# Loading the output projection's inputs during the last attention heads of a perceiver block

## The reference

```python
x = x + xattn(layernorm(x), ctx, ctx, ...)   # 16 heads of 64; out = einsum(attn, Wo) + bo
x = x + attn(layernorm(x), ...)              # 8 heads of 64; 20 rounds of row and column normalisation of the logits
x = x + ffn(layernorm(x), ...)               # 8 experts, top-1 routing with a capacity of 161 rows
```

## Time and profile before

| what | us |
|---|---|
| median of 3 runs | 3321.17 |
| lowest and highest | 3320.79, 3326.48 |
| the profiled execution | 3323.82 |
| its span in the profile | 3322.1 |
| PE busy | 3094.8 (93%) |
| DVE busy | 1755.2 (53%) |
| ACT busy | 1453.4 (44%) |
| POOL busy | 116.5 (4%) |

### The profile page before, as it was taken

The page is one execution under the profiler, slowest core; times in us unless marked ns, Lnnn a source line. Parts: engine busy times, 40 slices in busy tenths (PEclk is TensorE's granted clock), DMA queues, the critical chain, the costliest instruction groups (busy, mean ns, idle before and its releaser), DMA issues. The chain is left out here.

```text
span 3322.1 us, 62803 instructions
## 1 busy us (share of the span) xinstructions
PE 3094.8 (93%) x25686; PEld 2701.5 (81%) x25686; DVE 1755.2 (53%) x3257; ACT 1453.4 (44%) x2994; POOL 116.5 (4%) x87
## 2 busy tenths in 40 slices
PE   6899999999999999999999999999879679869997
PEld 5688888888888888888888888888736579859997
DVE  5355656565565555556555555655523788740001
ACT  3355555555555555555555555555512510011111
POOL 0000000000000000000000000000040320100001
PEclk9899999999999999999999999999989755579998
DMA  7311221121121112112112111211080000217761
GB/s 304 118 40 38 74 63 45 55 76 38 51 74 57 42 57 67 38 51 74 57 44 67 57 51 44 74 43 38 10 192 7 16 33 0 78 50 275 252 238 59
DMA packets 234789, 253.16 MB, mean 76 GB/s; under 512 B 22296, under 2 KB 169912, under 8 KB 234064
## 3 DMA queue, kind: packets, MB, share of 16 engines
q1 hardware_dynamic: 233008, 241.79, 22.8%
q0 software_dynamic: 1280, 4.20, 0.4%
q10 hardware_dynamic: 288, 4.19, 0.3%
HBM read 215.42 MB, written 34.70 MB: 75 GB/s over the span
## 5 line engine op out<-in xcount | busy, mean ns | idle before, releaser
L216 PE MATMUL fills<-wv_group,ctxT_hi 128*128 128x256 f32 x4096 | 799.5, 288 | 1.3 <-DVE ctxT_lo L421 0.6
L224 PE MATMUL fills<-ctxT_hi,wk_pairs 128*128 128x512 f32 x2048 | 704.9, 405 | 0.7 <-DVE keys L436 0.7
L216 PEld LDWEIGHTS fills<-wv_group,ctxT_hi 128*128 128x128 f32 x4096 | 655.3, 191 | 24.2 <-issue 21.0
L436 DVE SCALAR_TENSOR_TENSOR keys<-fills,bk,keys 64x512 fp32r<-64x512 f32 x512 | 383.8, 750 | 412.1 <-ACT keys L353 408.4
L216 PE MATMUL fills<-wv_group,ctxT_lo 128*128 128x256 f32 x2048 | 579.4, 283 | 0.0
L353 ACT ACTIVATE keys<-fills,bk 64x512 fp32r<-64x512 f32 x512 | 350.0, 684 | 408.3 <-PE fills L224 405.0
L224 PEld LDWEIGHTS fills<-ctxT_hi,wk_pairs 128*128 128x128 f32 x2048 | 387.8, 189 | 103.7 <-issue 23.8
L429 DVE TENSOR_TENSOR values<-fills,values 128x512 fp32r<-128x512 f32 x256 | 176.9, 691 | 435.7 <-ACT values L348 435.7
L224 PE MATMUL fills<-ctxT_lo,wk_pairs 128*128 128x512 f32 x1024 | 403.5, 394 | 0.0
L216 PEld LDWEIGHTS fills<-wv_group,ctxT_lo 128*128 128x128 f32 x2048 | 392.7, 192 | 0.0
L473 DVE TENSOR_TENSOR probsT<-probsT_ps,probsT 128x512 fp32r<-128x512 f32 x504 | 348.3, 691 | 66.3 <-ACT probsT L385 57.1
(11 more groups left out here) (211 smaller groups left out, 3105.5 us busy)
## 6 DMA issues: line engine op xcount, KB each, us to landing
e_w<-in_L_ffn_W SPq DMA_DIRECT2D x64, 1024.0 KB, 8.7
ctx_stage<-in_ctx SPq DMA_DIRECT2D x128, 256.0 KB, 2.9
wv_group<-wv_split SPq DMA_DIRECT2D x64, 512.0 KB, 4.6
wk_pairs<-wk_split SPq DMA_DIRECT2D x128, 256.0 KB, 3.2
q<-q_split SPq DMA_DIRECT2D x256, 64.0 KB, 2.7
q_split<-p_qb SPq DMA_DIRECT2D x16, 512.0 KB, 3.5
o_parts<-o_half SPq DMA_DIRECT2D x128, 64.0 KB, 1.5
a_ua<-o_parts SPq DMA_DIRECT2D x32, 256.0 KB, 6.6
```

The lines of the kernel that those rows point to most:

```text
L216: last = nc.tensor.matmul(pJ[:, bank[0], 256 * k:256 * k + 256], c[:, t, s:s + P], wv[:, w, t, :], start=t + n == 0, stop=t == DT - 1 and ...
L224: last = nc.tensor.matmul(pJ[:, bank[0], :], wk[:, p, w, t, :], c[:, t, 512 * j:512 * j + 512], start=t + n == 0, stop=t == DT - 1 and n == 2)
L436: last = nc.vector.scalar_tensor_tensor(out=keys[lo_rows(j), x, 512 * j:512 * j + 512], in0=pJ[DK * a:DK * a + DK, bk_, :], scalar=bk_sb[h ...
```

## The change

The context's place in SBUF becomes a region of its own (`shared`), from which a new class `Early` takes buffers that are used once the last fill has been made: `Wo`, the three raw weights of the self-attention (each in its own buffer now), two buffers of `a_ua` and two of the sums `a_us`. The row scales and `xbv` have places outside of it. SP issues `early_loads` in the last group of heads, and GpSimd adds the first two batches during the heads. In the projection's block the remaining sums are made two batches ahead, and the waits are split accordingly. `q_sb` and `k_sb` move to the next block, since the region is given back only after the projection. Semaphores are cleared, with a barrier, after the logits instead of after the whole self-attention.

```diff
+class Early:
+    def __init__(self, nc, offset, left, sem):
+        at = lambda n, shape, words: nc.alloc_sbuf_tensor_at(n, shape, F32, offset=offset + 4 * words)
+        self.xo = at("a_xo", [P, XH // 2, D], 0)
+        self.w = at("a_w", [P, 3, DT, D], 4096)
+        self.ua = at("a_ua", [P, 2, 2, XH // 2, P], 10240)
+        self.us = at("a_us", [P, 2, XH // 2, P], 14336)
...
+    def add(self, nc, pool, b):
+        pool.wait_ge(self.u_in[b % 2], 64 * (b // 2 + 1))
+        nc.gpsimd.tensor_tensor(self.us[:, b % 2, :, :], self.ua[:, b % 2, 0, :, :], self.ua[:, b % 2, 1, :, :],
+                                ALU.add).then_inc(self.added, 1)
...
                         h = 4 * g + i
+                        if last and g == XG - 1:
+                            early_loads(b, i)
...
+            def early_loads(b, i):
+                if i == 0:
+                    sp.wait_ge(filled, PRO + PER * b + fill_no(16 * XG - 17, True) + 1)
+                    for n in range(2):
+                        sp.wait_ge(o_out[n], 128 * 2 + 16)
+                    for n in range(2):
+                        early.u_load(sp, o_parts, n)
+                    sp.dma_start(early.xo[:, :, :], xo.rearrange("(a u) k d -> (u k) a d", u=2)).then_inc(early.xo_in, 16)
+                    sp.wait_ge(scale_out, 16 * batches)
+                    with nc.allow_non_contiguous_dma(reason="one number per token and head; the bias, once"):
+                        sp.dma_start(early.rs[:, 0:B - 1, :], row_scale[0:B - 1].rearrange("b t h -> t b h")).then_inc(early.rs_in, 16)
+                        sp.dma_start(early.xbv[:, :], x_bv.rearrange("(a u) k -> (u k) a", u=2)).then_inc(early.xo_in, 16)
+                    for n in range(3):
+                        sp.dma_start(early.w[:, n, :, :], aw[n].rearrange("(t p) d -> p t d", p=P)).then_inc(early.w_in, 16)
+                if i >= 2:
+                    sp.wait_ge(early.added, i - 1)
+                    for n in range(2):
+                        sp.wait_ge(o_out[n], 128 * (i + 1) + 16)
+                    early.u_load(sp, o_parts, i)
...
+        @block.gpsimd
+        def _(pool):
+            for b in range(2):
+                early.add(nc, pool, b)
...
                 @block.gpsimd
                 def _(pool):
+                    weights_lo(0)
                     for b in range(B):
-                        pool.wait_ge(u_in[b % 2], 64 * (b // 2 + 1))
-                        if b:
-                            pool.wait_ge(merged, b)
-                        nc.gpsimd.tensor_tensor(us[:, :, :], ua[:, b % 2, 0, :, :], ua[:, b % 2, 1, :, :],
-                                                ALU.add).then_inc(added, 1)
+                        if b + 2 < B:
+                            pool.wait_ge(merged, b + 1)
+                            early.add(nc, pool, b + 2)
...
-                        if b in (3, 5, 7):
+                        if b in (1, 3):
+                            weights_lo((b + 1) // 2)
...
                 @block.scalar
                 def _(act):
-                    act.wait_ge(rs_in, 16)
                     for b in range(B):
+                        act.wait_ge(early.rs_in, 16 if b < B - 1 else 32)
...
+            shared_space.close()
...
+        nc.clear_and_free_semaphores(used)
+        nc.all_engine_barrier()
+        used.clear()
         bo_sb = sb("s_bo", [P, D], F32)
...
-            nc.clear_and_free_semaphores(used)
-            nc.all_engine_barrier()
-            used = []
             weights.make(1)
```

More of the change, by code:

```diff
@@ L23 @@
 EPS = 1e-5
+SBUF_END = 229344
 def new_semaphore(nc, name, used):
@@ L29, in new_semaphore, with u_load, cross_attention @@
     return used[-1]
-def cross_attention(nc, ctx, wk_split, wv_split, q_split, bk, ident, o_parts, row_scale, used, batches=B):
+class Early:
[5 more added lines that the diff above has]
+        self.us = at("a_us", [P, 2, XH // 2, P], 14336)
+        self.rs = left("a_rs", [P, B, XH])
+        self.xbv = left("a_xbv", [P, XH // 2])
+        self.xo_in, self.rs_in, self.w_in, self.added = (sem(n) for n in ("a_xo_in", "a_rs_in", "a_w_in", "a_added"))
+        self.u_in = [sem("a_u_in0"), sem("a_u_in1")]
+    def u_load(self, sp, o_parts, b):
+        for n in range(2):
+            for u in range(2):
+                sp.dma_start(self.ua[DK * u:DK * u + DK, b % 2, n, :, :],
+                             o_parts[b].rearrange("(a u) k t -> u k a t", u=2)[u, DK * n:DK * n + DK, :, :]
+                             ).then_inc(self.u_in[b % 2], 16)
+    def add(self, nc, pool, b):
+        pool.wait_ge(self.u_in[b % 2], 64 * (b // 2 + 1))
+        nc.gpsimd.tensor_tensor(self.us[:, b % 2, :, :], self.ua[:, b % 2, 0, :, :], self.ua[:, b % 2, 1, :, :],
+                                ALU.add).then_inc(self.added, 1)
+def cross_attention(nc, ctx, wk_split, wv_split, q_split, bk, ident, o_parts, row_scale, shared, early, xo, x_bv, aw, used,
+                    batches=B):
     NS = 4
@@ L808, in _ @@
                 def _(sp):
[L809 to L815, removed]
@@ L816, in _, with row @@
-                    u_load(0)
-                    sp.dma_start(xo_sb[:, :, :], xo.rearrange("(a u) k d -> (u k) a d", u=2)).then_inc(xo_in, 16)
+                    def row(out, src, done):
+                        sp.dma_start(out[:, :], src.rearrange("(a d) -> a d", a=1).to_broadcast([P, D])).then_inc(done, 16)
+                    row(xbo, x_bo, xb_in)
+                    for hf in range(2):
+                        sp.dma_start(x1[:, 4 * hf:4 * hf + 4, :], x[4 * hf:4 * hf + 4].rearrange("b p d -> p b d")).then_inc(xs_in, 16)
@@ L824, in _ @@
[L824 to L833, removed]
@@ L834, in _ @@
-                    sp.wait_ge(w_in, 48)
+                    row(bvb, bv, c_in)
+                    for b in range(4, B):
+                        sp.wait_ge(early.added, b - 1)
+                        early.u_load(sp, o_parts, b)
+                    sp.wait_ge(c_in, 48)
                 @block.tensor
@@ L859, in _ @@
                         for a in range(XH // 2):
-                            last = nc.tensor.matmul(pY[:, b % 2, :], oT[:, b % 2, a, :], xo_sb[:, a, :],
+                            last = nc.tensor.matmul(pY[:, b % 2, :], oT[:, b % 2, a, :], early.xo[:, a, :],
                                                     start=a == 0, stop=a == XH // 2 - 1)
@@ L1806, in perceiver @@
         prepare(nc, x, xWq, xbq, xWk, xWv, ident, wk_split, wv_split, q_split, used)
-        cross_attention(nc, ctx_1024, wk_split, wv_split, q_split, xbk, ident, o_parts, row_scale, used)
+        shared_space, small = ExitStack(), ExitStack()
+        shared_space.enter_context(nc.sbuf_tensor("shared", [P, 2 * DT * S], F32, side="right"))
+        shared = SBUF_END - 4 * 2 * DT * S
+        early = Early(nc, shared, lambda n, shape: small.enter_context(nc.sbuf_tensor(n, shape, F32)),
+                      lambda n: new_semaphore(nc, n, used))
+        cross_attention(nc, ctx_1024, wk_split, wv_split, q_split, xbk, ident, o_parts, row_scale, shared, early, xWo, xbv,
+                        (aWq, aWk, aWv), used)
         with ExitStack() as kept:
```

61 lines of the change are left out of this document (27 added, 34 removed).

## The result

The changed kernel takes 3281.13 us (median of 4 runs, 3278.18 to 3285.63), the kernel before 3322.78 on the same chip (4 runs, 3320.79 to 3326.48): a ratio of 0.9875, with a 95% interval of 0.9857 to 0.9892. The profiled execution of the changed kernel took 3278.18 us (span 3276.5, mean clock 0.935; before 3322.1 and 0.930).

A forecast was written before the change was run, and what follows sets the result against it. TensorE was taken to limit the output projection, after three holes left by late transfers. Gains of 12.4 and 5.3 less 4.2 us made 13.5 off 3323.82, 3310.3; set against the median shown, forecast 3308 us, range 3302 to 3316.

The forecast's parts named there:

- the part on the rest: Moved semaphore clearing, ScalarE's weight copies, smaller loads and new buffer places, together taken to cost 0 us.
- The front: Output projection, opening to second spread of scales: loads already there, so 12.4 us gained, bounds 7.1 to 15.1.
- The projections: Eight projections, second spread to last projection's end: no hole left, 67.2 to 61.9 us, gain 5.3 us.
- the row: Output projection's waits: a_oT waited 33.9 us for the sums a_us before; forecast: sums always done before their product.
- The first subtraction ahead of the sum: GpSimd's 4.5 us weight subtraction precedes the third sum, done about 2425; product needs it at 2434, so no loss.
- The stall: Last heads: early loads hold head 11's store, head 13's addition is 5.2 us late, cost 4.2 us, bounds 0 to 8.6.
- the working: Calculation for head 11's store: 7.46 MB at 281 GB/s take 26.6 us, landing at 2402.1; VectorE's slack 1.02 us.
- the rival of no stall: Last heads: loads in by 2397 or passed by the store, all 17.7 us gained, 3303.5 us; chance 0.20.
- The moved barrier: Semaphore clearing moved from self-attention's end to after the first row sums' logarithm: gives and costs 0 to 4.4, taken 0.
- The crawl: Early loads among the heads: short pieces hold the queue at 120 GB/s, 62 us, a loss of 21, 3342 us; chance 0.07.
- The prediction's 281 GB/s: Transfer rate assumed for the 7.46 MB up to head 11's store, from the window at 2468: 26.6 us.

The follow-up runs named there:

- both repairs: Changed kernel with the three raw weights loaded behind batch 2's loads and 192 bytes of padding ahead of probsT: 3270.43 us, ratio 0.9851 to the kernel before.

## Why the prediction was wrong

**The step that failed** is one clause in the part on the rest: "the buffers' new places cost nothing while TensorE is the limit". It took the place of a buffer for something that has no time, and put neither a price nor a bound on it. No rival had it either, so the range was too narrow by the whole effect. It is shown by a pair of runs that change nothing but places: the distance of the change put into before gives 32.5 us, and the old distance put into the change takes the time to 3307.77. That this is 0.2 us from the forecast of 3308 is in part luck: the runs of that kernel spread over 5 us, the kernel before was 2.4 us faster on that chip, and in its trace 4.9 us that nobody forecast (`c_pLT` to the experts, 374.4) stand against 3.2 more up to the last fill (2376.1). The two parts add up: 12.6 + 32.5 = 45.1 us, where the change gained 41.6 and 43.9 in its two comparisons. The clause was also wrong in its reason. TensorE was busy for 1993 of the 2030 us from 250 to 2280, so little stood free to cover a matmul that starts 4 to 7 ns later: 26.1 us of the stretch to the last fill went, where the spacing gives 23 and the clock's falls 4.7.

**The front** was right in kind: 13.7 us gained, 12.4 forecast. ScalarE started 0.03 us after SP's first load (2393.00 against 2392.97) where 0.1 was assumed. From the first spread to the second 9.36 us passed (2394.09 to 2403.45) where 10.6 were forecast, since the low clock cost less: it was there until about 2397, 3 us, and not for 5.4 us of work as before.

**The projections**: 61.2 us without a hole, 61.9 forecast. The sums kept ahead. The waits of the stage show none of `a_oT` for `a_us`, which was the row; GpSimd now waits instead, for VectorE:

```profile
POOL a_us L55 <- DVE a_oT L934: 8.5, 3, 4.2
```

The first subtraction ahead of the sum did no harm, as argued.

**The stall** was the best term: a late addition at head 13, by 5.2 us as forecast and 6.5 as measured, for 4.2 and 4.3 us. A wait longer by 1.3 us at the same cost means that more slack stood behind it than the 1.02 us of the working, so the close agreement is partly luck. The store landed 30.0 us after the last fill's end (2376.8 less 2346.8, by the end of the wait), the working had 29.2 (its 2401.1 lets SP begin 0.1 us after the fill, which it does not say). Part of the mechanism was different: SP came to the store only 20 us after the last fill, since it stood while it issued what is ahead (4.92 us for one load of weights), and the queue then took 9.9 us; the working had put it all on the transfers. The changed kernel without the weights ahead shows no wait at all, so the rival of no stall was a matter of 3 MB.

**The moved barrier** was taken at 0 out of -4.4 to +4.4. At its new place the logarithm of the sums ends at 2569.67 and SP's next load comes at 2571.11:

```profile
2569.41 0.26 ACT L1074 ACTIVATE s_ls<-s_rowsum 128x64 f32<-128x64 f32 x1
2571.11 0.37 SPq L1171 DMA_DIRECT2D s_wo<-in_L_attn_Wo  x1
```

so it costs some 1.4 us there, and the stretch grew by 1.3. At the old place, for the earlier trace rows, 2.9 us now lie between the last scatter's issue and the load, where 4.4 lay:

```profile
2939.75 0.96 POOL L1424 DMA_INDIRECT expert_rows<-g_xn,e_slot  x1 [0.30 <-issue]
...
2943.61 0.34 SPq L1674 DMA_DIRECT2D f_eb<-expert_rows  x1
```

The two about cancel. The 4.9 us of the stretch that holds it are not shown to be the change's: kernels with the old barrier place ranged from 373.7 to 379.3 us there, those with the new one from 374.1 to 377.7. The barrier was not tried by itself, nor were the sums two batches ahead without the early loads.

**The crawl** did not come. The loads ahead of the store, with 7.46 MB, were in after 30.0 us, an average of 249 GB/s. By the transfers' own view, in 40 slices of 1.5 us from 2340, the rate sinks for two slices only, when the row scales in 64-byte pieces and `a_xbv` in 4-byte pieces are under way:

```profile
GB/s 0 0 0 5 0 74 255 201 201 200 208 205 217 378 388 397 120 39 341 339 384 344 350 372 270 202 200 237 200 198 156 43 0 0 49 7 160 236 336 384
```

The reader can see three rates in it: some 200 GB/s for the `a_ua` loads (rows of 512 bytes), 339 to 397 for `a_xo` and the weights (rows of 2048 bytes), 120 and 39 for the scales and `a_xbv`. So the mechanism of this rival did show, but for 3 us. The prediction's 281 GB/s, with 2.5 us for landing and short pieces, came out near the mean of a mix that it had not seen, which is luck too.

## What to carry to other kernels

A change that moves buffers can move every matmul that reads them: before trusting any comparison, put the old distance of the operands back into the new kernel, or the new one into the old, as a control. Where a kernel is bound by long rows of matmuls from the same two buffers, a pad of 64, 128 or 192 bytes between them is a cheap experiment, to be tried for each value: here 192 was worth more than the work that was planned, 64 gave 7 us and 128 nothing clear of noise. And loads put ahead of a store in one queue cost that store both the engine's issue time and the transfers, 20.0 and 9.9 us here: with only two buffers behind it VectorE waited, and with the bulk behind the store it did not.

## What the hardware showed that was not expected

The start-to-start time of two fp32r matmuls with 256 moving columns went with the distance of `wv_group` and all behind it from the context: 120 ns for most at 0 and 512 bytes, 118 at 64 and 320, from 115 to 122 at 128, 113 and 114 at 192. Why 192 is better than 64, and what in the memory or in TensorE it is, stays open.

VectorE's addition for head 12 takes 1.09 us, against 0.28 to 0.29 for the others, and GpSimd adds two halves at that time:

```profile
2360.05 2.39 POOL L55 TENSOR_TENSOR a_us<-a_ua 128x1024 f32<-128x1024 f32 x1 [3.02 <-DMA a_ua<-o_parts]
```

GpSimd's sum ends at 2362.44 and the addition at 2362.58, 0.14 us behind it; in the kernel with later weights they end at 2361.98 and 2362.13, in the change run again at 2360.85 and 2361.00. With both repairs the addition takes 1.97 us, and again ends 0.15 us behind the sum. So the addition did not run beside the sum but behind it. The Trainium skill (SBUF — State Buffer, section SBUF: two separate sides) says that VectorE, in an operation with two operands from that memory, and GpSimd share a pair of ports which one of them holds for a whole instruction; these traces agree. It cost VectorE 0.8 us once, and 1.7 with both repairs; what that did to the end of the heads was not measured by itself.
